# First loads reordered, six products ahead of the first scores, GpSimd adding the self attention's offset, and the experts' first layer in f16 halves

## What is computed

```python
x = x + L0_xattn(_layernorm(x), ctx_512, ...)   # causal self attention + cross attention, 16 heads of 8
x = x + L0_ffn(_layernorm(x), ...)
x = x + L1_xattn(_layernorm(x), ctx_512, ...)   # two _mha (16 heads of 32): self, then cross
x = x + L1_ffn(_layernorm(x), ...)              # mixture of 8 experts, top 1, capacity 640

# inside _mha: q, k, v of normed inputs, softmax(q k^T), causal mask after it, then
x_out = x + o @ li1_w + li1_b
h = gelu(_ln(x_out) @ li2_w + li2_b)
return x_out + h @ li3_w + li3_b

# inside L1_ffn, per expert e over its (up to) 640 tokens
hdn  = relu(einsum('ecd,edf->ecf', buf, w1) + b1)      # d = 128, f = 512
eout = einsum('ecf,efd->ecd', hdn, w2) + b2
```

## Time and profile before

| | us |
|---|---|
| median of 3 runs (range) | 1431.26 (1430.59 to 1431.32) |
| the profiled execution | 1433.22 |
| its span | 1431.5 |
| TensorE busy | 1334.5 (93%) |
| VectorE, ScalarE, GpSimd busy | 988.8, 844.7, 653.8 |

### The profile page before, as it was taken

The page is one execution under the profiler, slowest core; times in us unless marked ns, Lnnn a source line. Parts: engine busy times, 40 slices in busy tenths (PEclk is TensorE's granted clock), DMA queues, the critical chain, the costliest instruction groups (busy, mean ns, idle before and its releaser), DMA issues.

```text
span 1431.5 us, 42872 instructions
## 1 busy us (share of the span) xinstructions
PE 1334.5 (93%) x17912; PEld 871.1 (61%) x17912; DVE 988.8 (69%) x2236; ACT 844.7 (59%) x1325; POOL 653.8 (46%) x1118
## 2 busy tenths in 40 slices
PE   6899999998999999989999999898989999999995
PEld 3455555554455554456667666665766777777685
DVE  6688887875555555678988988764578887875232
ACT  3677777775666665567677776653466666531231
POOL 4455555533001003255666665443347775455254
PEclk8899999998999999999999999999999999998998
DMA  7000000000500000000000000111011111122441
GB/s 224 3 3 3 3 3 3 3 3 2 147 24 0 1 1 1 1 2 18 32 32 18 33 32 18 33 42 49 1 32 46 47 47 47 48 90 84 147 147 33
DMA packets 55186, 53.78 MB, mean 38 GB/s; under 512 B 9305, under 2 KB 49245, under 8 KB 54738
## 3 DMA queue, kind: packets, MB, share of 16 engines
q1 hardware_dynamic: 51154, 44.24, 10.2%
q0 software_dynamic: 2816, 6.11, 1.2%
q10 hardware_dynamic: 1024, 0.69, 0.2%
HBM read 20.34 MB, written 14.49 MB: 24 GB/s over the span
## 4 chain that ended last, share of the span: by engine, by line
PE 72%; DVE 11%; DMA 4%; SPq 3%; ACT 3%; issue 3%; POOL 2%; another core or an unknown queue 0%; ACTq 0%; POOLq 0%; DVEq 0%
PE psum L1552 5%; PE psum L1215 4%; PE psum L941 4%; PE psum L942 4%; PE psum L943 4%; PE psum L1179 3%; PE psum L1580 3%; DVE a_nm L603 3%; PE psum L2589 2%; PE psum L2564 2%; DVE b_nm L1635 2%; SPq L795 2%; PE psum L521 2%; DMA a_QT<-a_nmT 2%; PE psum L2033 2%
## 5 line engine op out<-in xcount | busy, mean ns | idle before, releaser
L1635 DVE TENSOR_REDUCE b_nm<-psum 128x4 f16<-128x1024 f32 x128 | 157.2, 1228 | 44.8 <-PE psum L1557 44.6
L720 ACT ACTIVATE a_prob<-psum 128x768 f32<-128x768 f32 (+1 forms) x160 | 136.2, 853 | 63.5 <-PE psum L458 61.8
L603 DVE TENSOR_REDUCE a_nm<-psum 128x4 f16<-128x1024 f32 (+1 forms) x96 | 117.2, 1223 | 42.1 <-PE psum L488 29.3
L772 POOL TENSOR_SCALAR_AFFINE_SELECT a_prob<-a_prob 128x512 f32<-128x512 f32 x128 | 82.4, 644 | 125.7 <-ACT a_prob L720 125.4
L171 POOL TENSOR_TENSOR f_ln_rstd<-f_ln_tmp,pow_half 128x4 f32<-128x4 f32 x24 | 25.4, 1058 | 202.2 <-DVE f_ln_tmp L160 202.1
L1069 ACT ACTIVATE xo_sb<-psum,f_w_h_s 128x512 f32<-128x512 f32 x64 | 44.1, 689 | 85.5 <-PE psum L943 85.5
L1552 PE MATMUL psum<-b_QTh,b_KTh 32*128 32x256 f16 x512 | 70.6, 272 | 14.9 <-DVE b_nm L1635 12.7
L1557 PE MATMUL psum<-b_KTh,b_QTh 32*128 32x256 f16 x512 | 70.8, 273 | 0.0
L1552 PE MATMUL psum<-b_QTh,b_KTl 32*128 32x256 f16 x512 | 69.7, 267 | 0.0
L1552 PE MATMUL psum<-b_QTl,b_KTh 32*128 32x256 f16 x512 | 69.6, 267 | 0.0
L1557 PE MATMUL psum<-b_KTh,b_QTl 32*128 32x256 f16 x512 | 69.6, 269 | 0.0
(11 more groups left out here) (449 smaller groups left out, 4657.5 us busy)
## 6 DMA issues: line engine op xcount, KB each, us to landing
f_h_wh<-b_rden SPq DMA_DIRECT2D x64, 128.0 KB, 2.2
f_h_wh<-c_rden SPq DMA_DIRECT2D x64, 128.0 KB, 2.1
expert_in<-empty SPq DMA_DIRECT2D x8, 662.5 KB, 11.4
m_xt<-expert_in SPq DMA_DIRECT2D x7, 662.5 KB
m_w<-in_L_ffn_w_dram SPq DMA_DIRECT2D x16, 256.0 KB
x_sb<-in_x_dram SPq DMA_DIRECT2D x8, 256.0 KB, 4.2
f_w_h_w<-in_L_ffn_h_w_dram SPq DMA_DIRECT2D x2, 1024.0 KB, 7.4
out_dram<-m_send SPq DMA_DIRECT2D x8, 256.0 KB, 2.5
```

The source lines that it names most:

```text
L603: nc.vector.tensor_reduce(out, psum[:, banks, :].rearrange("p i (a b) -> p i a b", a=groups), X, ALU.max, negate=True).then_inc(max_done, 1)
L720: nc.scalar.activation(prob[unit % 5][:, :, 0:width], psum[:, first:first + 2, 0:width], ACT.Exp, scale=SCALE).then_inc(exp_done, 1)
L772: nc.gpsimd.affine_select(out=diagonal, in_=diagonal, compare_op=ALU.is_ge, fill=0.0, base=0, pattern=[[0, 4], [1, P]], channel_multiplier ...
L1635: v.tensor_reduce(self.nm[:, :, :].rearrange("p t (j r) -> p j t r", r=32)[:, 2 * e:2 * e + 2, :, g], self.pr.psum[:, 2:4, :].rearrange("p ...
```

## The change

**First loads.** The table of ctx is issued first on ACT's queue. `wload` counts four weights (Wq, Wcq, Wk, Wck), a new semaphore `bload` their four biases, `wrest` the other seven loads. "qk0" waits for `wload`, VectorE's bias addition for `bload`, "ck" for neither of the rest; "v" waits for `wrest`.

**Products ahead of the first scores.** `tensor_warm(pr, 4, 6)` issues six products of 128x512 into a bank that nobody reads, ahead of the first wait for `nm_placed`.

**Self attention.** `vector_output` becomes one operation, xo += res. GpSimd writes xo = u + li1_b before it (`gpsimd_biased`, slot 20). `xo_done` counts once a batch in stage b (`OUTS`). VectorE's reciprocal stands one slot earlier (13 for 14), the normalising of the input one slot earlier (-26 for -25) and so does the other's (-20 for -19).

**Experts.** `tensor_hidden` makes three f16 products for each half. ACT casts the weights and the tokens to f16 (`scalar_turn`, after the second relu of the expert before), VectorE subtracts to get the low halves (`vector_weights`, `vector_turn`). w1 and b1 get a third buffer, and their load for n+2 is issued one expert earlier, ahead of the load of w2.

```diff
-    for i, x in enumerate("q cq k v".split()):
+    nc.scalar.dma_start(pr.ctxT[:, :, :], io["ctxT"]).then_inc(pr.ctxT_in, 16)
+    for i, x in enumerate("q cq k".split()):
         pr.load(Wcat[:, i, :], io["L0_xattn_W" + x], wload)
-        pr.load(bcat[:, i, :], io["L0_xattn_b" + x].partition_broadcast(P), wload)
-    nc.scalar.dma_start(pr.ctxT[:, :, :], io["ctxT"]).then_inc(pr.ctxT_in, 16)
-    for i, x in enumerate("ck cv".split()):
-        pr.load(Wctx[:, i, :], io["L0_xattn_W" + x], wrest)
-        pr.load(bctx[:, i, :], io["L0_xattn_b" + x].partition_broadcast(P), wrest)
+        pr.load(bcat[:, i, :], io["L0_xattn_b" + x].partition_broadcast(P), bload)
+    pr.load(Wctx[:, 0, :], io["L0_xattn_Wck"], wload)
+    pr.load(bctx[:, 0, :], io["L0_xattn_bck"].partition_broadcast(P), bload)
+    pr.load(Wcat[:, 3, :], io["L0_xattn_Wv"], wrest)
...
         if u == 0:
+            if n == 0:
+                tensor_warm(pr, 4, 6)
             nc.tensor.wait_ge(nm_placed, 64 * (n + 1))
...
-    VECTOR = {"rden": 14, "scaled": 16, "output": 23, 0: -28, 1: -25, 2: -22, 3: -19}
-    EARLY = {"o": 15, "rden": 9, "scaled": 12, "output": 16}
+    VECTOR = {"rden": 13, "scaled": 16, "output": 23, 0: -28, 1: -26, 2: -22, 3: -20}
+    EARLY = {"o": 15, "rden": 9, "scaled": 12, "biased": 13, "output": 16}
...
-        v.tensor_tensor(out, self.res[:, :, :], self.row2("li1_b"), ALU.add).then_inc(self.xo_done, 1)
-        v.wait_ge(self.xo_done, 2 * n + 1)
-        v.tensor_tensor(out, out, self.tokens(self.pr.u, n), ALU.add).then_inc(self.xo_done, 1)
+        v.wait_ge(self.biased, n + 1)
+        v.tensor_tensor(out, out, self.res[:, :, :], ALU.add).then_inc(self.xo_done, 1)
...
+    def gpsimd_biased(self, n):
+
+        self.nc.gpsimd.tensor_tensor(self.tokens(self.pr.xo, n), self.tokens(self.pr.u, n), self.row2("li1_b"),
+                                     ALU.add).then_inc(self.biased, 1)
...
-        for half in range(2):
-            inst = nc.tensor.matmul(psum[:, b + half, 0:HALF], w1[p][:, m * P:m * P + P],
-                                    xT[p][:, half * HALF:half * HALF + HALF], start=True, stop=True)
+        cols = slice(m * P, m * P + P)
+        for i, (w, x) in enumerate(((w1h, xTh), (w1l, xTh), (w1h, xTl))):
+            if m == 0 and i == 2:
+                nc.tensor.wait_ge(xT_out, n + 1)
+            for half in range(2):
+                inst = nc.tensor.matmul(psum[:, b + half, 0:HALF], w[p][:, cols],
+                                        x[p][:, half * HALF:half * HALF + HALF], start=(i == 0), stop=(i == 2))
...
+    def vector_weights(n):
+        nc.vector.wait_ge(w1_high, n + 1)
+        nc.vector.tensor_tensor(w1l[n % 2][:, :], w1[n % 3][:, :], w1h[n % 2][:, :], ALU.subtract).then_inc(w1_low, 1)
...
+    def scalar_turn(n):
+
+        high = xTh[n % 2]
+        nc.scalar.wait_ge(first_in, 32 * (n + 1))
+        nc.scalar.activation(w1h[n % 2][:, :], w1[n % 3][:, :], ACT.Copy).then_inc(w1_high, 1)
+        nc.scalar.wait_ge(xT_full, n + 1)
+        nc.scalar.activation(high[:, 0:N4], psum[:, 0, :], ACT.Copy)
+        nc.scalar.activation(high[:, N4:CAP], psum[:, 1, 0:CAP - N4], ACT.Copy).then_inc(xT_high, 1)
...
+                if m == 1 and n + 1 < E:
+                    scalar_turn(n + 1)
```

66 lines of the change are left out of this document (41 added, 25 removed).

## The result

| | before | after |
|---|---|---|
| median of 5 runs (range), us | 1431.26 (1429.65 to 1436.13) | 1419.22 (1417.26 to 1424.25) |
| the profiled execution, us | 1433.22 | 1417.90 |
| its span, us | 1431.5 | 1416.2 |

The ratio of after to before is 0.9901, with a 95% interval of 0.9879 to 0.9923: about 14 us faster (11 to 17); the two medians differ by 12.0. The forecast was 1417.2, with a range from 1408.5 to 1424. So the time came out as forecast, but the four terms behind it did not come out alike: part A's was too small, part B's hardly there, part C's too small and put down to the wrong edit, and part D's depends on late signals that some executions have and others haven't.

The account below looks back on a forecast made before the run. The prediction took TensorE, busy for 93% of the span, as the bound. Its terms 1.3 + 1.5 + 6.6 + 4.7 = 14.1 us, taken from 1431.3, gave 1417.2 us, with a range from 1408.5 to 1424.

Parts of the forecast that it names:

- part A: First loads: the second q/k product no longer stands behind ck's wait; 1.3 us gained, bounds 0 to 2.5.
- part B: Layer 0's first scores: six products in TensorE's wait keep the clock up; 1.5 us gained, bounds 0 and 1.7.
- part C: Self attention: VectorE's new slots and GpSimd's addition end waits for the maxima; 6.6 us gained, bounds 1 and 8.5.
- part D: Experts: f16 products shorten each hidden block, 0.75 us net an expert; 4.7 us gained, bounds 0 and 6.5.
- the excess: Layer 0: first to second row-maxima DMA takes 21.51 us, the next distance 19.79; the 1.72 between was put to half clock.
- recurring wait of 0.61: Self attention: scores wait for VectorE's maxima in ten of sixteen batches; ending it gains 6.1 us.
- 0.72 at the change of stage: After the self attention: GpSimd's addition for batch 15 delays the rstd; costs 0.72 us, bounds 0 and 1.8.
- margins that the text called thin: Self attention: VectorE's later maxima were counted to have 0.1 to 0.2 us left at the tightest slot.
- the rival built on it: Self attention: VectorE's operations wait on GpSimd's 16 additions through the port lock; 1434.8 us, 0.23% slower; chance 0.06.
- The last expert's three blocks: End of the experts: three hidden blocks, each 0.25 us shorter, gain 0.75 us.
- The tail's stall goes: Last expert products: their 4.54 us wait and half clock end, 6.4 us more gained, 1410 to 1411; chance 0.13.
- The experts become ACT's: Experts: third relu and outputs wait for ACT's casts, leaving about 1 us of gain there; 1421 us, chance 0.12.

Follow-up runs that it names:

- e9: The changed kernel without GpSimd's 30 indirect stores of experts 1 to 6; ratio to the kernel before 0.9898.
- e12: The changed kernel with the first loads of the kernel before; ratio to the kernel before 0.9928.
- e7: The kernel before with only VectorE's other slots in the self attention, both additions staying on VectorE; ratio to the kernel before 0.9954.
- e4: The kernel before with only the experts' first layer in f16 halves; ratio to the kernel before 1.0004.
- e5: The whole changed kernel run again, on the second chip; ratio to the kernel before 0.9947.

## Why the prediction was right, and where it wasn't

**The number.** 1417.2 was forecast and 1419.22 measured. On the second chip the same kernel gained only 0.53% (8 us), and there part D gives next to nothing. That the number fitted to 2 us is in part luck: errors of both signs in the terms, and a pair of executions in which the late signals stood in before and not in after. The sum of the four terms is right; the lower of the two sums of bounds, given as 2, is 1 (0 + 0 + 1 + 0), which changes nothing else.

**Part A** had the mechanism right (ck's wait was in the way of the second q/k product) and the size too small: 2.1 to 2.5 us instead of 1.3 at equal clock. The step that failed is the choice of the middle "since no row prices the new queue order": the first bias addition came 0.65 earlier and everything behind it 2.6. What was missed is that the half clock at the start, seen in the earlier trace rows as a product of 1.65, has two lengths. In the first profile the longer one (3.8 to 4.0 more) took back more than the edit gave.

**Part B** had the cause of the excess right and its own effect wrong: 0.5 us instead of 1.5. The step that failed is the one that "if they keep the granted clock at 1.00 the excess goes" takes for granted. The six products didn't keep it: the clock fell to 0.50 in all eight traces with them, in six only behind the first scores, in two (e9, e12) just ahead of the products, which then ran at 0.50 and cost 0.9 to 1.05. Where it was back at 1.00 from the first scores on (e9), the excess was gone (19.82 against 19.79).

**Part C** was right in its main step: the recurring wait of 0.61 went in all ten batches, and the batch came out at 21.1 as forecast. The sum was too small, 6.6 against 8.8, in two terms. By the distance between two batches' output projections, the ten regular batches gave 6.9 instead of 6.1 (two of them had been 22.09 and not 21.72), and the last four 2.6, where 1.24 was forecast for the reciprocal one slot earlier. The 0.72 at the change of stage came as 0.71 and stands behind the stage's 9.6. The margins that the text called thin held: no other slot's maximum took the wait's place. What the forecast got wrong about C is who earns it. It weighed GpSimd's addition at length; e7 shows that the slots alone do all, and the addition only costs its 0.7 behind the end of the stage.

**The shared port.** The rule of the Trainium skill cited in the prediction (page "SBUF — State Buffer", section "Who interferes with whom") and the trace agree again: VectorE's addition, with two inputs in SBUF, takes 0.412 at best and 0.890 in the median of the 16, and each of the eleven long ones meets a GpSimd subtraction that reads SBUF. But the rival built on it didn't come: VectorE was busy for 18.27 of a batch after, never near TensorE's 21.0, the 0.5 us that it loses to the port stand where nobody waits, and GpSimd's sixteen additions took 0.73 at most.

**Part D** had the period right: 8.67 against the 8.71 that follows from 9.46 less 0.75, with a bubble for the relu as forecast (0.16 idle by the record). Two steps failed. "The last expert's three blocks" don't count where the stores set the end; what is left to reach the end measured 4.5. And the relu's lateness behind the third hidden block, which stood in the earlier trace rows as an idle time of 3.38, was not looked at: the f32 blocks had been covering it. In e4 and e5, on the first two chips, it left 1.0 us of the 4.5, and the times show no gain.

**The rivals.** "The tail's stall goes" did happen in the first measurement, and was given 0.13; whether it is the change's doing is open (e5 has it back; e9 to e12 haven't). "The experts become ACT's" gave the right size on two chips for another reason. The forecast of the time held because part A was 1 and part C 2 us better and the tail's stall was away, against part B, the start's long half clock and the rest of what the stretch ahead of the self attention lost.

## What to carry to other kernels

When an engine's work is late by a fixed amount each round, try the order of its steps before moving work to another engine: one line of slots gave 9.6 us here, the moved addition nothing. Before shortening an engine's stage, ask what its old length covered (a late signal, a chain of stores behind it), and work out the end from the chain that ends last, not from the engine that is busiest. And run each part alone: a sum that comes out right can be made of terms that don't.
